# One ring of four accumulator banks for row scores and general products, and ten phases a batch instead of twenty units

## Time and profile before

| | us |
|---|---|
| three runs | 1256.14, 1258.88, 3407.16 |
| median | 1258.88 |
| profiled execution | 1255.18 |
| its span, first to last instruction | 1253.4 |
| PE / DVE / ACT / POOL busy in the span | 1126.7 / 835.4 / 677.8 / 472.8 |
| mean granted TensorE clock (1 is 2.4 GHz) | 0.961 |

### The profile page before, as it was taken

How to read it: one execution, slowest core, us unless ns; L and a number is a source line. 1 busy time by engine, 2 the same in 40 slices (tenths; PEclk the granted TensorE clock), 3 DMA queues, 4 the chain that set the end, 5 groups by cost and what they waited for, 6 DMA issues and landing times.

```text
span 1253.4 us, 27298 instructions
## 1 busy us (share of the span) xinstructions
PE 1126.7 (90%) x8462; PEld 787.5 (63%) x8462; DVE 835.4 (67%) x1955; ACT 677.8 (54%) x1067; POOL 472.8 (38%) x536
## 2 busy tenths in 40 slices
PE   4467789999999999999999999999999999989876
PEld 3344456766666666766666666767666666656565
DVE  5497867575767776676767767675767677665332
ACT  1256647465564747465664747365655747474601
POOL 2231334435353444444253434444353434332311
PEclk8678879999999999999999999999999999999989
DMA  5745453645556454644556454645555565641201
GB/s 201 176 143 141 120 146 96 187 122 156 122 148 174 137 154 112 188 124 157 114 165 148 141 151 118 195 112 170 122 165 123 145 164 138 162 117 37 76 21 34
DMA packets 94983, 169.90 MB, mean 136 GB/s; under 512 B 14872, under 2 KB 36120, under 8 KB 94944
## 3 DMA queue, kind: packets, MB, share of 16 engines
q1 hardware_dynamic: 93888, 166.53, 49.3%
q10 hardware_dynamic: 832, 1.83, 0.4%
q0 software_dynamic: 224, 1.04, 0.2%
HBM read 92.28 MB, written 77.07 MB: 135 GB/s over the span
## 4 chain that ended last, share of the span: by engine, by line
PE 73%; DVE 17%; issue 6%; DMA 2%; ACT 2%; POOL 1%; DVEq 0%; POOLq 0%; SPq 0%; ACTq 0%
PE ps_m L516 24%; PE ps_m L659 18%; PE ps_m L629 9%; PE ps_t L601 9%; PE ps_s L558 5%; PE ps_m L638 5%; DVE m_raw L851 4%; PE ps_s L587 2%; DVE m_raw L846 2%; DVE stats L907 2%; DVE x_res L922 1%; DVE rope_in L870 1%; DVE m_pad L860 1%; DVE x1T_lo L878 1%; DVE mv L912 1%
## 5 line engine op out<-in xcount | busy, mean ns | idle before, releaser
L732 ACT ACTIVATE pT<-ps_t 128x512 f32<-128x512 f32 x640 | 345.9, 599 | 275.8 <-PE ps_t L601 275.4
L851 DVE TENSOR_REDUCE m_raw<-ps_s 128x1 f32<-128x512 f32 (+2 forms) x768 | 345.1, 504 | 158.6 <-PE ps_s L587 157.8
L993 POOL TENSOR_SCALAR_AFFINE_SELECT pT<-pT 128x512 f32<-128x512 f32 (+1 forms) x320 | 174.9, 551 | 418.2 <-ACT pT L732 416.0
L659 PE MATMUL ps_m<-w,gact 128*128 128x256 f32 x1024 | 240.4, 386 | 1.8 <-ACT gact L800 1.1
L659 PEld LDWEIGHTS ps_m<-w,gact 128*128 128x128 f32 x1024 | 188.6, 190 | 31.2 <-ACT gact L800 1.5
L558 PE MATMUL ps_s<-k_st,q_st 48*128 48x512 f32 (+3 forms) x1024 | 136.5, 324 | 42.9 <-DVE m_raw L851 24.3
L601 PE MATMUL ps_t<-q_st,k_st 50*128 50x512 f32 (+3 forms) x1024 | 169.0, 388 | 0.5 <-ACT pT L732 0.4
L629 PE MATMUL ps_m<-pT,v_aug 128*32 128x512 f32 (+3 forms) x2048 | 155.6, 445 | 6.5 <-DVE rope_in L870 3.0
L601 PEld LDWEIGHTS ps_t<-q_st,k_st 50*128 50x128 f32 x1024 | 82.1, 186 | 98.7 <-issue 89.4
L558 PEld LDWEIGHTS ps_s<-k_st,q_st 48*128 48x128 f32 x1024 | 95.3, 192 | 53.7 <-DVE m_raw L851 31.9
L629 PEld LDWEIGHTS ps_m<-pT,v_aug 128*32 128x32 f32 x2048 | 58.5, 111 | 83.2 <-issue 79.0
(11 more groups left out here) (112 smaller groups left out, 1582.3 us busy)
## 6 DMA issues: line engine op xcount, KB each, us to landing
qk_scr<-rot_hi SPq DMA_DIRECT2D x64, 512.0 KB, 3.6
q_st<-qk_scr SPq DMA_DIRECT2D x128, 192.0 KB, 4.7
k_st<-qk_scr SPq DMA_DIRECT2D x128, 192.0 KB, 5.2
qk_scr<-rot SPq DMA_DIRECT2D x32, 512.0 KB, 4.1
o_scr<-o_raw SPq DMA_DIRECT2D x64, 256.0 KB, 2.1
r_b<-in_xT SPq DMA_DIRECT2D x17, 512.0 KB, 8.0
o_c<-o_scr SPq DMA_DIRECT2D x32, 256.0 KB
r_b<-r_scr SPq DMA_DIRECT2D x32, 256.0 KB
```

The source lines that it names most:

```text
L659: mm = pe.matmul(pm[:, 0:D], gact[:, k, n * P:(n + 1) * P], w2[:, k, :], start=(k == 0), stop=(k == NHT - 1))
L732: act.activation(pT[:, g % 2, slot, half * T:(half + 1) * T], ps_t[:, ST_BANK[2 * n + r], :], ACT.Exp, scale=SCALE).then_inc(exp_done, 1)
L851: ins = dve.tensor_reduce(m_raw[:, r, u // 2, qt:qt + 1], ps_s[:, r, off:off + (qt + 1) * P], AX.X, ALU.max, negate=True)
L993: pool.affine_select(out=v, in_=v, compare_op=ALU.is_ge, fill=0.0, base=0, pattern=pattern, channel_multiplier=-1).then_inc(mask_done, 1)
```

## The change

1. **Banks.** `ps_s` and `ps_m` become one ring `ps_m` of four banks. Each `S` takes two in turn (r = 0, 1), each general product one. PE waits before each for the tile that last had the bank, by a list computed from the order of steps (`tiles`, `BANK`, `bank`); in the steady order that is the tile four places earlier, but for six tiles after the first `PV` of an iteration, where the ring is turned by two so that it closes.
2. **Phases.** Two units make one of ten row phases p: `early(p)`, then `S` 2p+8, `ST` 2p, `ST` 2p+1, `S` 2p+9, then `late(p)`, then both `SEL`. All general products stand in `early`. `W2` and `W2B` of one n follow each other.
3. **Rotation.** `rot` and `rot_hi` have a half for each of the two rotations of a batch, and only the first waits for sent data, that of the batch before. `ROPE` of batch 0 runs on DVE; `LOW` and `XLO` always run on POOL.
4. **Start.** The ones in `k_st` are set by POOL, not DVE. The low-rank additions to v, and v's split, come after those of q and k; PE starts QK without them and waits for them at the first `V`. ACT rounds x before it issues the two loads of the up tables. `BU`, `BD`, `EL` come earlier in the list, `UM` later; setup units come by twos and fours a phase. The low-rank products use `ps_t`.
5. **Semaphores.** `oc_in` and `rb_in` become one for each half.

```diff
+    def early(p):
+        if p == 0:
+            put("FILL", i, 3)
+            put("BIAS", i - 2, 0)
+            put("BIAS", i - 2, 1)
+            if static and i == -1:
+                gemm("QK", 0, 0)
+            gemm("QK", i + 1, 1)
+            gemm("W1", i - 2, 6)
+            gemm("W1", i - 2, 7)
+        elif p == 1:
+            put("XRES", i - 1, 0)
+            put("XRES", i - 1, 1)
+            put("HIGH", i + 1, 0)
+            put("LOW", i + 1, 0)
+            gemm("QK", i + 1, 2)
+            gemm("MT", i, 1)
+            put("QKH", i + 1, 0)
+            gemm("PV", i - 1, 3)
+            put("MROW", i, 1)
+            put("RAW", i - 1, 3)
+        elif p == 2:
+            put("VC", i)
+            gemm("QK", i + 1, 3)
+            put("QKL", i + 1, 0)
+            gemm("W2", i - 2, 0)
+        elif p == 3:
+            put("HIGH", i + 1, 1)
+            put("LOW", i + 1, 1)
+            put("QKH", i + 1, 1)
...
+            gemm("W2", i - 2, 1)
+        elif p == 4:
+            put("QKL", i + 1, 1)
+            gemm("MT", i, 2)
+            gemm("PV", i, 0)
+            put("ON", i - 1, 1)
+            put("FILL", i + 1, 0)
+            put("MROW", i, 2)
+            put("RAW", i, 0)
+            gemm("W2", i - 2, 2)
+        elif p == 5:
+            gemm("W2", i - 2, 3)
+            gemm("WO", i - 1, 0)
+            put("FILL", i + 1, 1)
+        elif p == 6:
+            gemm("WO", i - 1, 1)
+            put("LNS", i - 1, 1)
+            put("LNA", i - 1, 0)
+            if not static or i >= 0:
+                gemm("V", i + 1, 0)
+            gemm("MT", i, 3)
+            put("LNB", i - 1, 0)
+            put("LNB", i - 1, 1)
+            gemm("PV", i, 1)
+        elif p == 7:
+            gemm("XT", i - 1, 0)
+            gemm("XT", i - 1, 1)
+            if not static or i >= 0:
+                gemm("V", i + 1, 1)
+            gemm("W1", i - 1, 0)
+        elif p == 8:
+            for n in range(1, 5):
+                gemm("W1", i - 1, n)
+        else:
+            gemm("MT", i + 1, 0)
+            gemm("W1", i - 1, 5)
+            put("MROW", i + 1, 0)
+            put("RB", i, 0)
+            gemm("PV", i, 2)
+            gemm("QK", i + 2, 0)
+
+    def late(p):
+        if p == 0:
+            put("ROPE", i + 1, 0)
+            put("GE", i - 2, 1)
+        elif p == 2:
+            put("ROPE", i + 1, 1)
             put("SMOC", i - 1, 1)
+        elif p == 3:
             put("RCP", i - 1, 1)
             put("REC", i - 1, 1)
             put("RB", i - 1, 1)
+        elif p == 4:
             put("LNS", i - 2, 2)
+        elif p == 5:
+            put("XTL", i + 2, 0, B + 1)
             put("LNS", i - 2, 3)
+            put("LNS", i - 1, 0)
+        elif p == 6:
+            put("LNA", i - 2, 1)
+            put("MROW", i, 3)
+            put("RAW", i, 1)
+        elif p == 7:
+            put("LNB", i - 2, 2)
+            put("LNB", i - 2, 3)
             put("SMOC", i, 0)
+            put("XHI", i + 2, 0, B + 1)
+            put("FILL", i + 1, 2)
+            put("OUT", i - 2)
+        elif p == 8:
+            put("GE", i - 1, 0)
+            put("XLO", i + 2, 0, B + 1)
             put("RCP", i, 0)
             put("REC", i, 0)
+        elif p == 9:
+            put("RAW", i, 2)
+
+    for p in range(NU // 2):
+        early(p)
+        t, u = 2 * p, 2 * p + LEAD
+        ahead = [("S", i, u + k) if u < NU else ("S", i + 1, u + k - NU) for k in range(2)]
+        put(*ahead[0])
         put("ST", i, t)
+        put("ST", i, t + 1)
+        put(*ahead[1])
+        late(p)
+        put("SEL", i, t)
+        put("SEL", i, t + 1)
...
-        ps_s = pb("ps_s", [P, 2, T])
-        ps_m = pb("ps_m", [P, 2, T])
+        ps_m = pb("ps_m", [P, RING, T])
...
+        def rotate(eng, b, n):
+            eng.wait_ge(evac["QK"], 4 * b + 2 * n + 2)
+            if n == 0:
+                wait(eng, qk_out, QKN * b)
...
+                if kind == "S":
+                    wait(pe, max_done, 2 * (NU * b + n) + r + 1)
...
-            for r in range(2):
-                ins = dve.memset(k_st[ROWS * r + ROWS // 2:ROWS * (r + 1), :, :].bitcast(FP32), 1.0)
-            ins.then_inc(ones, 1)
+            for n in range(KD):
+                lora_in(n)
...
+            pool.memset(k_st[:, :, :].bitcast(FP32), 1.0).then_inc(ones, 1)
```

The setup table after the change, as (batch, phase, kind, first, count):

```diff
+    [(-1, 3, "BU", 0, STAGES_IN - 1), (-1, 5, "EL", 0, 2), (-1, 3, "BD", 0, STAGES_IN - 1),
+     (0, 0, "UM", 0, 4), (0, 1, "UM", 4, 4), (0, 2, "ZL", 0, 1)] +
+    [(0, 2 + k, "XU", 2 * k, 2) for k in range(6)] + [(0, 8, "XB", 0, 1)] +
+    [(0, 8 + k, "UT", 2 * k, 2) for k in range(2)] +
+    [(0, 8 + k, "XD", 2 * k, 2) for k in range(2)] + [(1, k, "XD", 4 + 2 * k, 2) for k in range(4)] +
+    [(1, 4 + k, "DM", 4 * k, 4) for k in range(2)])
```

More of the change, by code:

```diff
@@ L61, in put @@
             out.append((kind, b, n))
[L63 to L88, removed]
@@ L90, in steps, with gemm @@
-    for t in range(NU):
-        if t == 0:
-            put("FILL", i, 3)
-        if t < 2:
-            put("BIAS", i - 2, t)
-        if 2 <= t < 4:
-            put("XRES", i - 1, t - 2)
-        for at, b, n in ((3, i, 1), (8, i, 2), (13, i, 3), (18, i + 1, 0)):
-            if t == at:
-                put("MROW", b, n)
-        if t == 4:
+    def gemm(kind, b, n):
+        put(kind, b, n)
+        if kind == "W2":
+            put("W2B", b, n)
+            put("W2E", b, n)
+        if kind in ("MT", "PV"):
+            put({"MT": "MOUT", "PV": "OE"}[kind], b, n)
@@ L164, in steps @@
-        if t == 8:
-            put("FILL", i + 1, 0)
-        if t == 10:
-            put("FILL", i + 1, 1)
-        if t == 11:
-            put("LNS", i - 1, 0)
-            put("XTL", i + 2, 0, B + 1)
-        if t == 15:
-            put("XHI", i + 2, 0, B + 1)
-            put("FILL", i + 1, 2)
-        if t == 16:
-            put("XLO", i + 2, 0, B + 1)
-        if t == 18:
-            put("OUT", i - 2)
-        if t == 19:
-            put("ON", i, 0)
-        put("SEL", i, t)
-        for when, at, kind, n, count in SETUP_UNITS:
-            if t == at:
-                for k in range(n, n + count):
-                    setup(when, kind, k)
+        elif p == 9:
+            put("RAW", i, 2)
@@ new lines, in steps @@
+    for p in range(NU // 2):
[3 more added lines that the diff above has]
+        put(*ahead[0])
+        put("ST", i, t)
+        put("ST", i, t + 1)
[3 more added lines that the diff above has]
+        put("SEL", i, t + 1)
+        if p == NU // 2 - 1:
+            put("ON", i, 0)
+        for when, at, kind, first, count in SETUP_UNITS:
+            if static and (i, p) == (when, at):
+                for k in range(first, first + count):
+                    out.append((kind, 0, k))
@@ L553, in one @@
                         pe.wait_ge(fill[g], FILLN * (b + 1))
-                    wait(pe, max_done, 2 * (NU * b + n))
+                    scores = [ps_m[:, bank(kind, b, n, r), :] for r in range(2)]
                     def s_mm(r, off, x, qt, start):
                         rows, pr = slice(ROWS * r, ROWS * r + NK), GP * g + x
-                        return pe.matmul(ps_s[:, r, off:off + (qt + 1) * P],
+                        return pe.matmul(scores[r][:, off:off + (qt + 1) * P],
                                          q_st[rows, pr, qt * P:(qt + 1) * P],
@@ L871, in one @@
                        .then_inc(evac["QK"], 1)
+                elif kind == "ROPE" and rotates_on(b) == nc.vector:
+                    rotate(dve, b, n)
                 elif kind == "MT":
```

185 lines of the change are left out of this document (74 added, 111 removed).

## The result

The changed kernel is slower: 1342.3 us median of four runs (1330.1 to 1345.7), 1.0635 times the time before (as means, 1340.1 against 1260.1) with a 95% interval of 1.0537 to 1.0734. One execution of the kernel before, 3407.16 us, is left out of the ratio. The profiled execution took 1345.7, its span 1344.0, which is 90.6 more than the 1253.4 of before. The prediction was 1261, the range 1222 to 1300.

What follows compares the result with a forecast made beforehand. PE's work and its waits were taken as the bound. A full batch was 64.3 + 2.6 + 2.8 + 0.6 + 1.3 = 71.6 us; 1255.2 - 18 + 22 = 1259, predicted as 1261 with the median's offset, range 1222 to 1300.

Steps and rivals of the forecast that it cites:

- the last term of SP's queue: Full batch: ST 10 waits for MROW, now queued behind QKL and FILL; 1.3 us a batch, between 0 and 3.
- MROW behind FILL decides: Rival: QKL and FILL hold SP longer, ST 10 waits 4 us a batch; 74.3 a batch, 1297 us; chance 0.20.
- The rival on the clock: Rival: ten gaps of a microsecond lower the clock in full batches; 74.2 a batch, 1296 us; chance 0.08.
- MT: Phases 1, 4 and 9: MT waits for DVE's reductions and split; 2.6 us a batch for 1.1 before.
- The layernorm chain: Second WO through LNB: XT, V and W1 wait for DVE's longer chain; 2.8 us a batch for 1.2 before.
- Pairing: PE in full batches: ten phases instead of 20 units bring busy time from 67.4 to 64.3 us.
- the ten entries and exits: PE in full batches: ten fewer entries and exits of general-product runs, 0.2 us each, saving 2.0 us.
- check of the work: PE's full batch before: products, entries and units added up to 67.3 us, against 67.4 busy.
- Banks: Phases 9 and 1: last S waits for its shared bank, 0.5 with the next product and 0.1; 0.6 us.
- The start: Before full batches: first score -6, then -7 to batch 0, batch 0 -5, batch 1 0; -18 us, -28 to -8.
- The tail: After the full batches: waits are the same chain of steps, 0 us, between -3 and +3.

Runs made afterwards that it cites:

- e1: Changed kernel with SP sending MROW(i, 2) and RAW(i, 0) before FILL(i+1, 0) in phase 4: 1293.7 us, ratio 1.0272.
- e4: Changed kernel with twelve unused 128x512 products added ahead of ST 10's wait for MROW: 1322.3 us, ratio 1.0506.
- e9: Changed kernel with e3's edits, BIAS behind ROPE, and the second layernorm's later steps moved to later phases: 1247.6 us, ratio 0.9897.
- e3: Changed kernel with MROW ahead of FILL and each MT behind the product that stood behind it: 1263.0 us, ratio 1.0024.

## Why the prediction was wrong

**The failed step is the last term of SP's queue, 1.3 us a batch for `ST` 10's wait, which measured 3.1.** The prediction walked it from the start of phase 3's block; in the profile after, that block starts at 612.19.

| station, us behind the block's start | predicted | measured |
|---|---|---|
| inverse done | 4.1 | 4.2 |
| RB issued | 7.2 | 7.2 |
| QKL issued | 7.9 | 7.9 |
| first FILL | 12.0 | 12.4 |
| MROW issued | 14 | 14.4 |
| ST 10 could start | 15.9 | 16.1 |
| maxima in q_st | 16 to 18 | 19.3 |

Every station is within about 0.4 except the landing. I gave a pair of transfers of 8 KB 2 to 4 us behind FILL's data, without a row for it; it took 4.8 from the start of its issue to the first ST. That the queue's data is what holds it is shown by the same transfer in e1: 2.0 us to landing ahead of `FILL`, 4.6 behind it. With 2.0 it would have been in q_st at 16.4, an estimate from the table, and ST 10 would have waited 0.3. The term of 1.3 (0 to 3) measured 3.1 in this batch and 2.9 as the mean of ten. The rival "MROW behind FILL decides" gave 18.8 us as the point from which it decides, and ST 10 could begin at 19.3: the mechanism that happened was this rival, at a chance of 0.20, and even its 1297 was too low.

**The second failure is that a wait was priced at its own length.** By waits alone the full batch would be 64.3 + 7.8 = 72.1, near the forecast's 71.6. It was 77.2, and of the 5.1 between them 3.9 are clock, the rest PE's work. The rival on the clock had it as a separate case with gaps of one microsecond, and set gaps of up to 2.8 of "batch 1" against it; the waits of before show 2.8 in batch 0 (clock 0.75) and at most 2.3 in batch 1 (0.86), so a wait of 3 us was beyond both. In fact it rode on the other rival: the long idle stretch before ST 10 brought the clock down behind it (0.66 over the ten microseconds from 629 to 639 is 6.8 of them at the lower level), and e4, which fills it, is at 1.00. The Trainium skill, TensorE: Matmul & The Clock Gate, section "A second HAM failure mode: psum-queue depth-cycling", tells of PE idling between groups of products and its clock oscillating; here the granted clock also goes down and up again in every batch (0.66 in 629 to 639, 1.00 in 612 to 618), but what set it off most was one wait for a transfer, not the banks. I should have joined the two: any rival with one wait of several microseconds needs the clock in its price.

**MT: nearly right.** 2.6 was predicted, 3.1 measured (31.5 in ten batches). The waits of phases 4 and 9 are 0.91 and 0.90 for 0.9 and 0.8; that of phase 1 is 1.24 for 0.9. Removing all three gave 24.0 us alone and 30.7 on top of e1, against 43 for 3.1 x 14: other waits took their place (`rope_in` 1.05 for 0.3).

**The layernorm chain: half of the term, until ST 10's wait is gone.** 2.8 was predicted (XT 1.5, V 0.2, W1 1.1). The changed kernel shows 1.3 (W1 0.75, `gact` 0.4, XT 0.15), because DVE catches up while PE stands at ST 10 and runs slowly behind it. Once that wait is gone, in e1, XT waits 1.8 and W1 0.4, with 0.4 for `gact`. Waits that share an engine hide each other here: they were added up as if independent, and that the term for this chain was 1.5 too large made up for a part of what ST 10's was too small. That is luck.

**Pairing: right in kind, about half in size.** PE's work went from 67.4 to between 65.5 and 66.2, not to 64.3, so 1.3 to 2.0 were saved for 3.1. The block is as predicted, 1.50 for 1.52: from start to start, `S` and `ST` together take 15.5 us a batch in e4, for 16.4 before. What failed are the ten entries and exits, 2.0 in the sum: all other products, without e4's useless ones, take 50.6 for 51.1 before. The sum's check of the work, 67.3 against 67.4, could not warn of this, because it closed by chance: it has 2.1 for a PV, and PV took 2.29 before and after:

```profile
587.03 2.36 PE L629 MATMUL ps_m<-pT,v_aug 128*32 128x512 f32 x32
589.32 0.55 PE L601 MATMUL ps_t<-q_st,k_st 50*128 50x128 f32 x4
```

Four of those are 0.8 us, which the check had put on other terms. Which of the entries saved nothing is not shown.

**Banks: right order of size.** 0.6 was predicted; S waits 0.3 for `rope_in`, and the first product behind it 0.2 for a row's reductions (the 0.4 of S for `gact` is counted above). The ring itself costs little in waits.

**The start: right until batch 0, wrong behind it.** The first score at 36.0 for 39.4, the first product of batch 0 at 50.95 for 51, `VC` 16.8 earlier. Batch 0 was to win 5 and batch 1 nothing; they lost 5.6 and 6.0, so -18 became -5.2. Batch 1 has the waits of the full batches in it (`m_pad` 7.3, `m_scr` 5.2), and in e9, with both edits of e3, it is back at 71.4. Batch 0 is 74.2 and more in e3 and e9 too; its part may be the setup moved into it or the table by twos, which stays open.

**The tail** gave +1.6 for 0, within what was allowed.

In sum: 14 batches were to cost 22, and 13 of them cost 94; -18 at the start became -5. Had ST 10's term been 3.1 and the clock's 3.9, the same sum would have given 71.6 + 1.8 + 3.9 = 77.3, for 77.2 measured. It comes out so well because two other errors cancel, the layernorm chain 1.5 too large and PE's work 1.2 to 1.9 too small.

## What to carry to other kernels

When a step is moved behind another in a queue that waits in order, walk to the landing of its transfer and not to its issue, and take the landing with the queue's data ahead of it; then place it where nothing ahead of it waits, or make sure that what is ahead of it is early. Price an idle stretch of several microseconds of TensorE at more than its length if the trace shows two clock levels, since the work behind it can run slow, and expect that taking out the longest wait uncovers the ones that it had hidden. A reordering that saves the matrix engine a few microseconds of entries is worth it only if each product that covered a hand-over before still covers one.
